# Preparing steps of an attention kernel: rows normalised and transposed one chunk further ahead, projection first on TensorE, squares first on ScalarE

## The reference

```python
h = W.T[x] + b + pe                                    # embedding and positions
# layer 1: linear-like attention, 8 heads of 16, with a running normalisation
hn = layernorm(h); q, k, v = hn @ w_qkv
dots = q @ k.T * scale, causal (0 above the diagonal)
mu, s = mean and variance of each row up to the diagonal
h = h + (((dots - mu) * rsqrt(s + eps)) * g + b, causal) @ v @ w_out + b_out
# layer 2: softmax attention, 2 heads of 64, then a gated mixture of 8 experts
hx = layernorm(layernorm(h)) * ln_g + ln_b
q, k = l2norm(hx @ Wq) * 8 * qn_g, l2norm(hx @ Wk) * kn_g;  v = hx @ Wv
y = softmax(causal(q @ k.T / 8)) @ v @ Wo
gate = softmax(y @ gate_W + gate_b)
h = h + sum_e gate_e * (gelu(y @ W1_e + b1_e) @ W2_e + b2_e)
```

## Time and profile before

| | us |
|---|---|
| median of 3 runs | 876.5 (875.99 to 876.71) |
| the profiled execution, its own time | 878.74 |
| its span | 876.9 |
| TensorE busy in the span | 797.4 (91%) |
| VectorE busy | 694.8 (79%) |
| ScalarE busy | 492.0 (56%) |
| GpSimd busy | 335.2 (38%) |

### The profile page before, as it was taken

One profiled execution on the slowest core, in us unless ns is written; L12 is line 12 of the kernel. 1 busy time (PEld: TensorE's weight loads), 2 busy tenths in 40 slices (PEclk: granted clock), 3 DMA queues, 4 the chain that ended last, 5 costly groups with the idle time before them and its releaser, 6 DMA issues.

```text
span 876.9 us, 21020 instructions
## 1 busy us (share of the span) xinstructions
PE 797.4 (91%) x8228; PEld 562.0 (64%) x8228; DVE 694.8 (79%) x1550; ACT 492.0 (56%) x1015; POOL 335.2 (38%) x379
## 2 busy tenths in 40 slices
PE   2699999999867789888999799999999999999997
PEld 1568877788533445555555456777777777777775
DVE  3558898888678656657677548899999999999997
ACT  2435555555345557767689875555555555555553
POOL 6639999777545547555567540000000000000000
PEclk9789999999889879999999979999999999999999
DMA  3100111000000000000000000000000000000000
GB/s 123 54 7 21 36 37 37 25 26 25 0 1 0 2 1 1 2 1 2 1 5 12 1 3 1 1 14 2 13 2 14 2 13 2 14 2 14 1 14 13
DMA packets 9634, 12.03 MB, mean 14 GB/s; under 512 B 1848, under 2 KB 6592, under 8 KB 9536
## 3 DMA queue, kind: packets, MB, share of 16 engines
q1 hardware_dynamic: 8512, 8.59, 3.3%
q0 software_dynamic: 1024, 2.10, 0.9%
HBM read 8.59 MB, written 2.10 MB: 12 GB/s over the span
## 4 chain that ended last, share of the span: by engine, by line
PE 79%; DVE 6%; ACT 5%; issue 5%; POOL 2%; DMA 1%; another core or an unknown queue 0%; DVEq 0%; ACTq 0%; POOLq 0%
PE ps L954 76%; DVE mx L813 2%; ACT room L547 1%; ACT room L540 1%; PE ps L1118 1%; DMA h_all<-emb_rows,idx 1%; POOL sm L264 1%; DVE room L907 1%; ACT hxT L470 1%; POOL ss L328 1%; ACT qh L488 1%; PE ps L982 0%; PE ps L962 0%; PE ps L1267 0%; PE ps L1246 0%
## 5 line engine op out<-in xcount | busy, mean ns | idle before, releaser
L562 ACT ACTIVATE cst<-ps,col 128x512 f32<-128x512 f32 x256 | 175.9, 689 | 162.2 <-PE ps L954 161.6
L954 PEld LDWEIGHTS ps<-arena,sq 128*128 128x128 f16 x3072 | 192.2, 98 | 61.9 <-DVE sq L938 4.1
L954 PE MATMUL ps<-arena,sq 128*128 128x128 f16 x3072 | 213.0, 219 | 0.8 <-DVE sq L938 0.7
L954 PE MATMUL ps<-y,arena 128*128 128x512 f16 x768 | 207.1, 379 | 1.3 <-DVE och L887 1.3
L938 DVE TENSOR_TENSOR sq<-cst,sq 128x512 f16<-128x512 f32 x256 | 175.9, 687 | 4.4
L362 POOL TENSOR_TENSOR room<-room 128x512 f16<-128x512 f32 (+3 forms) x119 | 118.8, 1013 | 100.1 <-ACT room L547 100.0
L813 DVE TENSOR_REDUCE mx<-ps 128x2 f32<-128x1024 f32 (+2 forms) x76 | 81.6, 1074 | 55.1 <-PE ps L954 55.0
L933 DVE CAST sq<-cst 128x512 f16<-128x512 f32 x256 | 108.9, 425 | 10.7 <-ACT cst L562 3.3
L540 ACT ACTIVATE room<-ps 128x512 f32<-128x512 f32 (+3 forms) x160 | 77.2, 539 | 45.8 <-PE ps L954 44.7
L954 PEld LDWEIGHTS ps<-v,room 128*128 128x128 f16 x1632 | 60.7, 100 | 42.8 <-issue 26.2
L954 PEld LDWEIGHTS ps<-y,arena 128*128 128x128 f16 x768 | 64.6, 98 | 33.1 <-issue 1.8
(11 more groups left out here) (154 smaller groups left out, 1154.4 us busy)
## 6 DMA issues: line engine op xcount, KB each, us to landing
sq<-w_rows SPq DMA_DIRECT2D x16, 256.0 KB
out<-h_all SPq DMA_DIRECT2D x32, 64.0 KB, 1.6
cst<-consts SPq DMA_DIRECT2D x1, 896.0 KB
h_all<-emb_rows,idx POOLq DMA_INDIRECT x32, 4.8
cst<-consts SPq DMA_DIRECT2D x1, 398.0 KB, 3.3
c<-consts SPq DMA_DIRECT2D x1, 256.0 KB
wqkv<-w_qkv SPq DMA_DIRECT2D x1, 192.0 KB
wsm<-w_sm SPq DMA_DIRECT2D x1, 192.0 KB
```

What stands on the lines that cost most here:

```text
L562: a.activation(hid[:, f], ps[:, HBANK[f], :], ACT.Gelu_apprx_tanh, bias=col[:, K_B1 + k:K_B1 + k + 1], scale=1.0 / WS).then_inc(S["hid_rea ...
L954: return t_.matmul(o, l, r, start=start, stop=stop, skip_group_check=True)
```

## The change

On TensorE a step begins with the projection of chunk c+2, which waits for `unit_qk(c)`, and `unit_T(c)` follows; the transposes of the normalised rows are those of chunk c+3 instead of c+2. On ScalarE squares come first, then `high_qk(c)`, then the affine copy for chunk c+3. On VectorE `normed2(c + 3)` stands where `normed2(c + 2)` stood, and the sum of squares and the low values of chunk c+2 (before: c+1) stand at the end of the step. GpSimd takes its factors a chunk earlier. Ahead of the steps the normalising of chunk 2 is added on all three engines, and `project2(0)` is cut in two: sample 0 where it was, sample 1 behind the first sample's products with dtm. Chunk 2's transposes go to bank 5. What is left of chunk 15 of the first attention moves by a step in places.

```diff
@@ -338,8 +338,10 @@
             l2_factors(0)
             both_norms(NT - 3)
             for c in range(NT):
-                if c + 1 < NT:
-                    l2_factors(c + 1)
+                if c == 0:
+                    l2_factors(1)
+                if c + 2 < NT:
+                    l2_factors(c + 2)
                 if c == 1:
                     coefs(NT - 1)
                 if c == 3:
@@ -497,14 +499,16 @@
                 sums_out(NT - 1, 1, b)
             ao_out(NT - 2)
             squares(1)
+            normed_T(2)
 
             def step_b(c):
+                if c + 2 < NT:
+                    squares(c + 2)
                 high_qk(c)
-                if c == 4:
+                if c == 3:
                     ao_out(NT - 1)
-                if c + 2 < NT:
-                    normed_T(c + 2)
-                    squares(c + 2)
+                if c + 3 < NT:
+                    normed_T(c + 3)
 
             for c in range(BTAIL):
                 step_b(c)
@@ -801,6 +805,7 @@
             low_v(0)
             stats2(NT - 3)
             outputs(NT - 2, 0)
+            normed2(2)
             dve.wait_ge(S["wlow_ready"], NEARLY)
 
             def row_max(it, r, kb, w, k, heads):
@@ -825,20 +830,21 @@
 
             def step_b(c):
                 unit_qk(c)
+                if c + 3 < NT:
+                    normed2(c + 3)
                 if c == 0:
+                    sum_squares(1)
+                    low_v(1)
                     h1_out(NT - 2)
-                if c == 5:
-                    h1_out(NT - 1)
-                if c + 2 < NT:
-                    normed2(c + 2)
-                if c + 1 < NT:
-                    sum_squares(c + 1)
                 if 0 <= c - 6 < 8:
                     single_max(c - 6)
                 if c:
                     low_qk(c - 1)
-                if c + 1 < NT:
-                    low_v(c + 1)
+                if c == 4:
+                    h1_out(NT - 1)
+                if c + 2 < NT:
+                    sum_squares(c + 2)
+                    low_v(c + 2)
                 if c == 1:
                     variances(NT - 1, 1)
                 if c == 2:
@@ -851,9 +857,7 @@
             for c in range(BTAIL):
                 step_b(c)
             unit_qk(NT - 2)
-            sum_squares(NT - 1)
             low_qk(NT - 3)
-            low_v(NT - 1)
 
             def out_part(m, j):
                 if j == 3:
@@ -1083,8 +1087,10 @@
                 if c == 1:
                     pe.wait_ge(S["sgc_ready"], 2 * NT - 2)
                 if c == 2:
+                    pe.wait_ge(S["x_sb"], 2 * NT - 1)
+                if c == 3:
                     pe.wait_ge(S["h1_ready"], NT - 1)
-                if c > 2:
+                if c > 3:
                     pe.wait_ge(S["hxT_sb"], c)
                 if c == 6:
                     pe.wait_ge(S["aoT_sb"], NT)
@@ -1094,7 +1100,7 @@
                     last = t_.transpose(ps[:, x2_bank(c), b * P:(b + 1) * P], x2[c % 2][:, b], ident)
                 last.then_inc(S["x2T_ps"], 1)
 
-            def project2(c):
+            def project2(c, samples=range(B)):
                 pe.wait_ge(S["hxT_sb"], c + 1)
                 if c == 0:
                     pe.wait_ge(S["qkv_sb"], 2 * NT)
@@ -1103,9 +1109,10 @@
                 if c >= 2:
                     pe.wait_ge(S["qkn_ready"], c - 1)
                     pe.wait_ge(S["vlo_ready"], c - 1)
-                for b in range(B):
+                for b in samples:
                     last = mm(ps[:, QB[c % 2] + b, 0:3 * D], hxT[c % 2][:, b], wsm[:])
-                last.then_inc(S["qkv2_ps"], 1)
+                if b == B - 1:
+                    last.then_inc(S["qkv2_ps"], 1)
 
             def unit_T(c):
                 pe.wait_ge(S["qkn_ready"], c + 1)
@@ -1127,7 +1134,7 @@
                 dots(cur, b, kT, qv)
                 sums(c, cur, b, state=False)
                 if b == 0:
-                    project2(0)
+                    project2(0, [0])
             normed_T(1)
             for b in range(B):
                 pe.wait_ge(S["dt_sb"], 2 * c + b + 1)
@@ -1135,14 +1142,16 @@
                     at = D + h * XW
                     last = mm(ps[:, 5 + b, at:at + XW], dtm[:, b, h], kv[cur][:, b, h], start=False)
                 last.then_inc(S["x_ps"], 1)
+                if b == 0:
+                    project2(0, [1])
             out_T(NT - 2)
             project2(1)
+            normed_T(2)
             out_project(NT - 2)
 
             def step_b(c):
-                unit_T(c)
                 if c + 2 < NT:
-                    normed_T(c + 2)
+                    pe.wait_ge(S["qkn_ready"], c + 1)
                     project2(c + 2)
                 if c == 3:
                     pe.wait_ge(S["hxT_sb"], 6)
@@ -1150,6 +1159,9 @@
                 if c == 4:
                     pe.wait_ge(S["hxT_sb"], 7)
                     out_project(NT - 1)
+                unit_T(c)
+                if c + 3 < NT:
+                    normed_T(c + 3)
                 if 0 <= c - 5 < 8:
                     row_scores((c - 5) // HS, (c - 5) % HS)
 
@@ -1410,7 +1422,7 @@
 
 
 def x2_bank(c):
-    return 1 if c == 0 else 7 if c == 1 else 0
+    return {0: 1, 1: 7, 2: 5}.get(c, 0)
 
 
 def on_pool(i):
```

## The result

The changed kernel takes 889.95 us (888.29 to 892.98, 4 runs) against 876.61 (875.99 to 878.8) for the kernel before: a ratio of 1.0138, 95% interval 1.0114 to 1.0162, slower by 13.3 us. The forecast was slower, 881.0, with 885.0 as the upper end. The direction was right, and so were the places where the time is lost; the size was forecast three times too small.

What follows compares the result with a forecast made beforehand. No engine is full; round trips of waits bound a step, 3.89 us before and after. Start +3.2, early steps +0.7, end -0.4, clock +1.0 sum to +4.5: 881.0 us, own range 878.5 to 883.5, wider 875.5 to 885.0.

Steps and rivals of the forecast that it cites:

- the late mask: Chunk 15's last mask on VectorE, behind the split first projection: at 226.45 instead of 222.40, 4.05 us late.
- the stall: Step 3: TensorE's out_T(15) waits for VectorE's outputs with other work queued behind; 2.4 us including the residual of chunk 15.
- One round trip is traded for another of the same length: Steady steps: the new loop over VectorE and the projection takes 3.89 us as before, so no gain per step.
- 0.05 to the next engine: Steady step: gap from unit_qk's end on VectorE to the projection on TensorE, 0.05 us.
- The start: First mask to unit_qk(1): the split projection 0 delays mask, outputs and projection 1; +3.2 us.
- P(1) is about 230.5: Start of projection 1 on TensorE, forecast at about 230.5 instead of 227.68.
- The early steps: unit_qk(1) to unit_qk(14): chunk 15's leftover VectorE work and a wait in step 3 enter the loop; +0.7 us.
- The clock: Projections 4 to 7 on TensorE: one runs at the lower clock, +1.0 us; bounds none (0) to three (+4).
- The end: unit_qk(14) to the second attention's first scores: 0.74 us instead of 1.10, -0.4 us.
- the forecast of 57.5 for unit_qk(1) to (14): Preparing steps: 13 x 3.89 plus 1.35, 1.92, 1.22 and 2.4 gives 57.5 us, against 56.8 before.
- the clock of the second attention: Rival: TensorE's clock stays up in the second attention's first 16 us, 5 us less, total 873.7; chance 0.12.
- The port lock: Rival: GpSimd's power blocks VectorE's pair of normalised rows; some +6 us more, 887; chance 0.03.

Runs made afterwards that it cites:

- e5: Changed kernel without the first of TensorE's two waits for the same unit rows ahead of project2(c+2): 889.32 us, ratio 1.0129 to the kernel before.
- e1: Changed kernel with project2(0) whole again at its old place, and a VectorE wait added ahead of normed2(3): 885.95 us, ratio 1.0089 to the kernel before.
- e6: Changed kernel with the rest of chunk 15 of the first attention moved to later places in the steps: 883.28 us, ratio 1.0085 to the kernel before.
- e12: The changed kernel itself, unedited, timed and profiled again: 893.21 us, ratio 1.016 to the kernel before.
- e4: Changed kernel plus products nobody reads, 32 in the start and 16 in each of steps 0 to 4: 887.93 us, ratio 1.0129; output not the reference's.
- e10: Changed kernel plus 16 products nobody reads in each of TensorE's steps 0 to 4, none in the start: 890.4 us, ratio 1.013.
- e2: Changed kernel with VectorE's sum_squares(c+1) right behind unit_qk(c), in place of sum_squares(c+2) later: 878.04 us, ratio 1.0004 to the kernel before.
- e8: Changed kernel with projection 0 whole, sum_squares(c+1) behind unit_qk(c), one unit-row wait, chunk 15's rest moved, high_qk(c) still ahead of hxT(c+3): 868.8 us, ratio 0.9918.

## Why the prediction was right in kind and wrong in size

The loops, the late mask and the stall were forecast as they came. What failed are the sizes of four terms of the sum: the clock (+1.0, about 4.1 measured), the gap between unit_qk and the projection (0.05, measured 0.24, 2.3 us over the steps), the start of projection 1 (1.4 later) and the stall (1.0).

- **"One round trip is traded for another of the same length"**: the loop was right, row by row (1.57, 0.63, 0.60 and 0.33 were measured, 1.59, 0.63, 0.60 and 0.33 forecast). Its first term was wrong. "0.05 to the next engine" came from the earlier trace rows, from another pair of engines and with the first of TensorE's waits holding and two behind it; 0.24 was measured, with three behind. e5 takes the doubled wait out and gets 0.10. Over 13 steps 0.18 is 2.3 us.
- **The start**: the mask was forecast 4.05 us late and is 4.3 later on the clock of its trace, 4.2 from the first mask. The step that failed is "P(1) is about 230.5", which was counted from VectorE's outputs alone. The second 16 small products start only behind the mask, ran at the lower clock, took 3.48, and ended at 231.5; the copy of their sums (231.53) is what projection 1 at 232.17 waited for. With it unit_qk(1) is 4.6 late and not 3.2; e1 gives back 4.6.
- **The early steps**: the extras behind low_v were near the forecast (unit_qk(1) to (2) is 5.43, 4.07 and 1.36 for the variances; the statistics of chunk 15 made their step 4.94, 0.87 more than 4.07, where 0.96 was forecast), and so was the stall's place. e6 gives 3.4 for it, where 2.4 was forecast.
- **The clock** was the most mis-sized term: "for P(4) to P(7) I put one such projection", +1.0, with +4 as the bound. Three of them ran at 2.90, each 1.37 more inside the loop, 4.1: the far bound. It was three in this profile; in e12, the same kernel, projection 4 took 1.67, so this term differs by 1.2 from one execution to the next. TensorE now waits 1.9 to 3.2 us in one piece ahead of projections 3, 4 and 5 (2.14 ahead of projection 5). With busy work in that piece projection 5 took 1.53, in both runs that had it (e4, e10); in the six profiles with VectorE's order as changed and no such work it took 1.88 to 2.90. For projection 6 no run shows it, and idle time alone does not settle the clock: ahead of projection 4 TensorE waited 3.24 us in both profiles of the changed kernel, and it took 2.90 and 1.67. The kernel before had slow projections in this stretch too (2.83 at 237.66, 2.65 at 247.72), so the 4.1 are set against the forecast, not against the kernel before.
- **The end**: -0.2 where -0.4 was forecast.
- Against the forecast of 57.5 for unit_qk(1) to (14), 64.57 was measured. Of the 7.1 (the clock term was not in the 57.5) 2.3 are the gap, 4.1 the clock and 1.0 the stall, together 7.4; of the 0.3 too much, 0.2 are the two times 0.09 that the statistics were shorter than forecast. The 2.0 us outside the stage were not forecast, and their cause stays open.
- **The rivals**: the clock of the second attention did not come back. The granted clock is 0.81 over its first 8 us and 0.74 over the next 20 in the changed kernel, 0.91 and 0.61 in the kernel before, and no time came back: from the first scores on, the changed kernel takes 586.0 us, the kernel before 584.2; over all runs here it is 583.6 to 586.0. The port lock did not happen: the pair of rows (L756) stands beside the power in every steady step and takes 0.59 to 0.60: at 280.43, for example, with the power from 279.95 for 1.64. (The 1.64 that the prediction gives with the earlier trace rows is not in those rows; the kernel before has it, at 278.19.) The pair takes 0.59 with GpSimd idle too (231.65 in the kernel before). The Trainium skill ("SBUF — State Buffer", section "SBUF: two separate sides") says that the later of the two would be blocked until the other's whole instruction is over, if VectorE is in a two-port mode; whether it is in one here no run shows, and no row of the steady steps shows a block.

## What to carry to other kernels

When a step's order is changed, write down every closed loop from one engine's instruction back to itself, with its gaps, before asking which engine is busy: here work was taken off one loop of 3.9 us and put on another of the same length, and only moving the sum of squares past unit_qk opened that one too (3.72, and 3.34 with hxT first on ScalarE as well). A part of an operation that carries the signal must not be moved behind work that waits for the signal's reader. Size the lower clock as a term of its own wherever the new order gathers TensorE's idle time, and take more than one profile before an edit is credited with a projection at the full clock: the same kernel had projection 4 at 2.90 and at 1.67.

## What the runs showed that was not expected

- A wait that is written twice is not free: without the doubled one the gap to the projection fell from 0.24 to 0.10 us (e5), and the step by 0.16 us. It shows behind hxT too: where hxT is what TensorE waits for, the gap is 0.10 with the doubled wait (e2) and 0.05 without (e8).
- Products of 34 columns slow down as wide ones do: 16 took 1.87 us in the first half of chunk 15 (granted clock 1.00 from 222.8 to 224.8) and 3.48 in the second (0.53 from 228.0 to 231.5).
- The part ahead of the stage, the same in all kernels, varies by up to 4.6 us between profiled executions (the first mask stands at 214.89 in e6 and at 219.51 in e2), so stages have to be compared from a mark of their own.
